# An adaLN transformer layer with circular-convolution attention and a mixture of experts: an opening and a last block in another order

## The reference, cut to what matters

```
mod = silu(c) @ wmod                     # sa, ca, ga, sb, cb, gb, each 4 x 256
ga, gb: sign kept, magnitude at least 0.25
h = layernorm(x) * (1 + ca) + sa
q, k, v = unit(h @ Wq.T + bq), unit(h @ Wk.T + bk), unit(h @ Wv.T + bv)   # unit: every Fourier coefficient divided by (its magnitude + 1e-8)
s = cumsum over tokens of fft(k) * fft(v)
x = x + ga * ifft(s * conj(fft(q)))
h = layernorm(x) * (1 + cb) + sb
gate = h @ gate_w;  top 2 of 8 experts, softmax weights
y_e = dense_2[e] @ swiglu(dense_1[e] @ h + b1[e]) + b2[e]                  # 512 hidden
x = x + gb * (weighted sum of the two y_e)
```

## Time and profile before

| | |
|---|---|
| median of 3 runs | 584.66 us (583.52 to 586.32) |
| the profiled execution: its time | 584.68 us |
| its span in the trace | 582.5 us |
| TensorE busy | 544.5 us, 93% of the span |
| VectorE busy | 473.1 us, 81% |
| ScalarE busy | 302.2 us, 52% |
| GpSimd busy | 282.8 us, 49% |

### The profile page before, as it was taken

The page is one execution under the profiler, slowest core; times in us unless marked ns, Lnnn a source line. Parts: engine busy times, 40 slices in busy tenths (PEclk is TensorE's granted clock), DMA queues, the critical chain, the costliest instruction groups (busy, mean ns, idle before and its releaser), DMA issues.

```text
span 582.5 us, 13330 instructions
## 1 busy us (share of the span) xinstructions
PE 544.5 (93%) x4008; PEld 404.8 (69%) x4009; DVE 473.1 (81%) x1062; ACT 302.2 (52%) x514; POOL 282.8 (49%) x197
## 2 busy tenths in 40 slices
PE   9999999999999985779899999999999999999992
PEld 5544555655656552537588888888888888888881
DVE  1267889999999989999688888888888888888882
ACT  4777688889797863654433333333333333333330
POOL 0004033343423342000638878877878877777634
PEclk9988999999899987858899999999999999999997
DMA  8314544644735437833677897786886686786533
GB/s 313 126 45 155 153 136 109 203 132 136 208 103 176 115 120 219 309 64 70 162 121 107 136 152 118 136 132 116 145 157 109 134 139 121 136 155 112 88 45 36
DMA packets 82109, 79.37 MB, mean 136 GB/s; under 512 B 45140, under 2 KB 71892, under 8 KB 81816
## 3 DMA queue, kind: packets, MB, share of 16 engines
q0 software_dynamic: 16912, 31.74, 31.3%
q1 hardware_dynamic: 63864, 46.28, 29.9%
q10 hardware_dynamic: 1296, 0.87, 0.5%
HBM read 44.06 MB, written 22.23 MB: 114 GB/s over the span
## 4 chain that ended last, share of the span: by engine, by line
PE 72%; DVE 13%; ACT 4%; issue 4%; DMA 4%; POOL 2%; POOLq 0%; DVEq 0%; ACTq 0%
PE ps L807 30%; PE ps L826 14%; PE ps L551 13%; PE ps L610 3%; DMA out_rows<-w_stage,region 3%; PE ps L652 2%; PE ps L564 2%; PE ps L648 2%; PE ps L474 1%; DVE region L1293 1%; POOL out_rows L1749 1%; ACT region L976 1%; PE ps L482 1%; ACT region L923 1%; DVE region L1415 1%
## 5 line engine op out<-in xcount | busy, mean ns | idle before, releaser
L807 PE MATMUL ps<-region,w_sb 128*128 128x256 f16 (+1 forms) x1920 | 194.3, 261 | 0.9 <-DMA region<-region 0.4
L807 PEld LDWEIGHTS ps<-region,w_sb 128*128 x1920 | 170.4, 98 | 20.1 <-issue 2.1
L1749 POOL DMA_INDIRECT out_rows<-w_stage,region x71 | 126.4, 1780 | 60.4 <-DMA out_rows<-w_stage,region 22.8
L1739 POOL DMA_INDIRECT region<-h_scratch,region x71 | 91.8, 1292 | 67.7 <-DVE region L1576 45.0
L1178 ACT ACTIVATE region<-region 128x1024 f16<-128x1024 f32 (+1 forms) x40 | 38.5, 961 | 130.4 <-DVE region L1630 130.4
L826 PE MATMUL ps<-region 128*128 x852 | 99.6, 273 | 1.9 <-DVE region L1636 1.7
L1622 DVE TENSOR_SCALAR region<-ps,region 128x256 f32<-128x256 f32 (+1 forms) x160 | 64.4, 448 | 43.0 <-PE ps L807 41.2
L826 PEld LDWEIGHTS ps<-region 128*128 128x128 f16 x852 | 82.6, 98 | 13.1 <-issue 3.5
L1166 ACT ACTIVATE region<-ps,region 128x256 f32<-128x256 f32 (+1 forms) x160 | 63.0, 445 | 53.0 <-PE ps L807 49.5
L551 PE MATMUL ps<-region 128*128 128x512 f32 x192 | 84.2, 595 | 3.2 <-ACT region L923 3.2
L1723 POOL TENSOR_TENSOR region<-region 128x512 f32<-128x512 f32 x30 | 37.3, 1270 | 94.9 <-DVE region L1320 94.9
(11 more groups left out here) (238 smaller groups left out, 702.3 us busy)
## 6 DMA issues: line engine op xcount, KB each, us to landing
w_stage<-in_w SPq DMA_DIRECT2D x20, 512.0 KB, 3.7
region<-in_x SPq DMA_DIRECT2D x8, 512.0 KB, 7.3
out_rows<-region SPq DMA_DIRECT2D x8, 512.0 KB, 3.0
h_scratch<-gb_bc SPq DMA_DIRECT2D x4, 1024.0 KB, 6.8
h_scratch<-region SPq DMA_DIRECT2D x8, 512.0 KB, 3.2
region<-region POOLq DMA_DIRECT2D x7, 512.0 KB, 4.5
region<-in_ramp SPq DMA_DIRECT2D x1, 2064.0 KB, 11.1
region<-in_w SPq DMA_DIRECT2D x4, 512.0 KB, 6.6
```

The source lines that it names most:

```text
L807: mm = pe.matmul(ps[:, GV + 2 * half + a, (f % 2) * MT:(f % 2) * MT + wide], w, xg_t[:, s, xa * KD + k, 0:wide], start=(n == 0), stop=(n = ...
L1739: G.indirect_dma_start(out=xg_rows[:, t % XG, u, :], out_offset=None, in_=h_scratch, in_offset=bass.IndirectOffsetOnAxis(ap=idx, axis=0)). ...
L1749: G.indirect_dma_start(out=out, out_offset=bass.IndirectOffsetOnAxis(ap=scatter_idx[:, at:at + 1], axis=0), in_=y_sb[:, t % 2, u, :], in_o ...
```

## The change

It rebuilds the opening (blocks 0 and 1) and reorders the last block.

- **Weights.** The first three chunks (EARLY = 3) are split by VectorE alone (`weight_chunk`: one scaling for the high part, one scale-and-subtract for the low). Their two ScalarE copies and six TensorE pieces go; `low_piece(0, i)` and `low_piece(1, 0)`, `(1, 1)` no longer exist. SyncE may load chunks 2 to 4 before the modulation table is written.
- **Block 0.** The magnitudes are added in three parts as the squares come (`first_magnitude`), the roots of k and v are taken between the copies (`first_root`), and VectorE adds the small constant. `modulation` runs after the `uk` product of `bind(0)` instead of before its reciprocal. ScalarE writes sb and 1 + cb already scaled by 8, which takes two VectorE instructions of `modulation` away.
- **Block 2** (the third) is normalised while block 0 is still being transformed; its transposes stand right behind `nyquist_sums(0)` on TensorE. `unbind(0)` now stands inside `bind(1)`, ahead of block 1's reciprocal; `project(1)` stands ahead of `modulation_rows` on TensorE, and `inverse(0)` behind both pieces that are left.
- **Last block.** TensorE adds x with two 512-column matmuls ahead of the wait for `unbind`; the high and low parts go to a buffer of their own (`last_parts`), so `last_split` waits for no store and no transposes; `last_residual(0)` comes before `split_rows(6)`, and `low_piece(8, 3)` and the splits of chunks 18 and 19 come later; VectorE does `last_moments(0)` before `low_rows(6)` and `top2(5)` after `last_low`. The masks of `picks` are set by GpSimd (`masks`), and the softmax weights are computed among the index steps.

The diff, cut to its core:

```diff
-            items += [("ny", 0, 0), ("lo", 0, 0)]
+            items.append(("ny", 0, 0))
+            continue
         elif t == 0:
-            items += [("pre", 0, 0), ("ny", 1, 0), ("row", 0, 0), *(("lo", 1, i) for i in range(4))]
+            items += [("ny", 1, 0), ("pre", 0, 0), ("lo", 1, 2), ("row", 0, 0), ("lo", 1, 3)]
...
-            for n in range(2):
+            for n in range(5):
                 load_weights(sp, n)
-            sp.wait_ge(mod_ready, 6)
+            sp.wait_ge(mod_ready, 4)
+            sp.wait_ge(mod_scaled, 2)
             sp.dma_start(mod_tab, mod_rows.bitcast(I32)).then_inc(mod_out, 16)
             sp.wait_ge(mod_out, 16)
             sp.dma_start(mod_bc.bitcast(I32), mod_tab[:, 0:3, :].partition_broadcast(P)).then_inc(mod_in, 16)
             sp.dma_start(gb_bc[:].bitcast(I32), mod_tab[0:2, 3, :].partition_broadcast(P)).then_inc(gb_in, 16)
-            for n in range(2, 6):
-                load_weights(sp, n)
+            load_weights(sp, 5)
...
+                if t == LAST:
+                    for h in range(2):
+                        pe.matmul(ps[:, OUT + h, :], ident_sb[:],
+                                  x_sb[:, t % XS, 2 * h:2 * h + 2, :].rearrange("p j d -> p (j d)"),
+                                  start=True, stop=False)
                 for j in range(TPB):
                     cols = ps[:, OUT + j // 2, (j % 2) * D:(j % 2 + 1) * D]
-                    if t == LAST:
-                        pe.matmul(cols, ident_sb[:], x_sb[:, t % XS, j, :], start=True, stop=False)
...
                     nyquist_cols(0)
+                    project(1)
                     modulation_rows()
-                    project(1)
-                    low_piece(0, 0)
+                    continue
                 elif t == 0:
                     transform(1)
+                    nyquist_cols(1)
                     nyquist_sums(0)
-                    nyquist_cols(1)
+                    project(2)
+                    low_piece(1, 2)
                     nyquist_row(0)
-                    low_piece(1, 0)
-                    low_piece(1, 1)
+                    low_piece(1, 3)
                     inverse(0)
-                    low_piece(1, 2)
-                    low_piece(1, 3)
                     continue
                 elif t + 1 < NBLK:
-                    project(t + 1)
+                    if t >= 2:
+                        project(t + 1)
...
-                low_piece(t + 1, 3)
+                if t < LAST:
+                    low_piece(t + 1, 3)
...
+            def modulation_rows(half):
+                act.wait_ge(mod_mm, half + 1)
+                act.wait_ge(unit_set, 2)
+                plain, scaled = ((0, 1), (3, 2))[half]
+                rows = ps[0:BATCH, OUT + half, :].rearrange("b (m d) -> b m d", m=2)
+                nc.scalar.activation(mod_rows[:, plain, :], rows[:, plain - 2 * half, :], ACT.Copy).then_inc(mod_copied, 1)
+                nc.scalar.activation(mod_rows[:, scaled, :], rows[:, scaled - 2 * half, :], ACT.Identity, scale=SX,
+                                     bias=scale_shift[0:BATCH, half:half + 1]).then_inc(mod_scaled, 1)
...
-                    if c == 2 and t == 1:
-                        split_weights(2)
                     act.wait_ge(z_ready, 6 * t + 2 * c + 2)
                     nc.scalar.activation(sq[:, c], z[:, t % 2, c, :, 0:BLK], ACT.Square).then_inc(sq_ready, 1)
+                    if t == 0 and c >= 1:
+                        first_root(c - 1)
+                    if t == 1 and c == 0:
+                        split_weights(EARLY)
                     if c == 0 and t >= 3:
                         residual(t - 2)
-                if t == 1:
-                    split_weights(3)
...
+            def first_root(c):
+
+                act.wait_ge(mag_part, c + 1)
+                nc.scalar.activation(mag[:, 0, c, 0:BLK], mag[:, 0, c, 0:BLK], ACT.Sqrt).then_inc(root_part, 1)
+
+            def first_roots():
+
+                act.wait_ge(ny_out, 1)
+                nc.scalar.activation(mag[:, 0, :, BLK:NB], mag[:, 0, :, BLK:NB], ACT.Sqrt).then_inc(root_part, 1)
+                act.wait_ge(mag_ready, 1)
+                nc.scalar.activation(mag[:, 0, QRY, 0:BLK], mag[:, 0, QRY, 0:BLK], ACT.Sqrt).then_inc(root_ready, 1)
...
-                act.wait_ge(h2_out, 16 * LAST)
-                act.wait_ge(tp2_done, KD * LAST)
-                nc.scalar.activation(h2_parts[:, 2 * h:2 * h + 2, HI, :], x2[:, 2 * h:2 * h + 2, :],
+                nc.scalar.activation(last_parts[:, 2 * h:2 * h + 2, HI, :], x2[:, 2 * h:2 * h + 2, :],
...
-                    split_weights(0)
-                    roots(0)
-                    split_weights(1)
-                    modulation_rows()
+                    first_roots()
                     spectra(1)
-                    low_piece(0, 0)
+                    modulation_rows(0)
+                    normal_rows(2)
+                    modulation_rows(1)
+                    continue
                 if t == 0:
-                    project(2)
-                    normal_rows(2)
-                    low_piece(1, 0)
-                    low_piece(1, 1)
+                    roots(1)
+                    low_piece(1, 2)
                     nyquist_row(0)
-                    roots(1)
+                    spectra(2)
+                    low_piece(1, 3)
+                    split_weights(4)
                     residual(0)
-                    low_piece(1, 2)
-                    low_piece(1, 3)
-                    spectra(2)
-                    split_weights(4)
                     split_weights(5)
                     continue
                 if t >= 2:
                     gate_rows(t - 2)
                 if t >= 1 and t + 2 < NBLK:
                     project(t + 2)
+                if t == LAST:
+                    low_piece(t + 1, 1)
+                    gate(t - 2)
+                    std2(t - 1)
+                    low_piece(t + 1, 2)
+                    nyquist_row(t)
+                    last_residual(0)
+                    split_rows(t - 1)
+                    last_residual(1)
+                    last_std(0)
+                    low_piece(t + 1, 3)
+                    split_weights(2 * t + 4)
+                    last_std(1)
...
+            def weight_chunk(n):
+
+                dve.wait_ge(w_in[stage_of(n)], 16 * arrivals(n))
+                hi, lo = parts_of(n)
+                V.tensor_scalar(hi, staged(n), SW, None, ALU.mult).then_inc(chunk_hi, 1)
+                dve.wait_ge(chunk_hi, n + 1)
+                V.scalar_tensor_tensor(out=lo, in0=staged(n), scalar=SW, in1=hi, op0=ALU.mult,
+                                       op1=ALU.subtract).then_inc(w_lo[n % 2], 2)
+
+            def first_magnitude(c):
+
+                dve.wait_ge(sq_ready, c + 1)
+                V.tensor_tensor(mag[:, 0, c, 0:BLK], sq[:, c, RE, :], sq[:, c, IM, :],
+                                ALU.add).then_inc(mag_part if c < QRY else mag_ready, 1)
...
+                if t == 0:
+                    dve.wait_ge(root_part, 3)
+                    V.tensor_scalar(mag[:, s, VAL, :], mag[:, s, VAL, :], EPS_UNIT, None, ALU.add).then_inc(eps_ready, 1)
                 dve.wait_ge(eps_ready, t + 1)
                 V.scalar_tensor_tensor(out=den, in0=mag[:, s, KEY, :], scalar=EPS_UNIT, in1=mag[:, s, VAL, :],
                                        op0=ALU.add, op1=ALU.mult).then_inc(den_ready, 1)
                 if t == 0:
-                    modulation()
+                    dve.wait_ge(root_ready, 1)
                 dve.wait_ge(den_ready, t + 1)
                 V.scalar_tensor_tensor(out=rec, in0=mag[:, s, QRY, :], scalar=EPS_UNIT, in1=den,
                                        op0=ALU.add, op1=ALU.mult).then_inc(all_ready, 1)
+                if t == 1:
+                    unbind(0)
                 dve.wait_ge(all_ready, t + 1)
                 V.reciprocal(rec, rec).then_inc(rec_ready, 1)
                 dve.wait_ge(rec_ready, t + 1)
                                 ALU.mult).then_inc(uq_ready, 1)
                 V.tensor_tensor(uk, z[:, s, KEY], mag[:, s, KEY, :].unsqueeze(1).to_broadcast([P, 2, NB]),
                                 ALU.mult).then_inc(uk_ready, 1)
+                if t == 0:
+                    modulation()
...
-            for t in range(-1, NBLK):
-                if 0 <= t < NBLK:
-                    bind(t)
-                if t >= 1:
-                    residual(t - 1)
-                if t >= 0 and t + 2 < NBLK:
+            ln1_rows(1)
+            ln1_moments(2)
+            for c in range(3):
+                weight_chunk(c)
+                if c == 0:
+                    ln1_rows(2)
+                first_magnitude(c)
+            bind(0)
+            magnitudes(1, slice(KEY, QRY))
+            magnitudes(1, slice(QRY, QRY + 1))
+            nyquist_apply(0)
+            for t in range(1, NBLK):
+                bind(t)
```

(40 more changed lines are left out.)

111 lines of the change are left out of this document (60 added, 51 removed).

## The result

The changed kernel takes 580.74 us (median of 11 runs, 580.04 to 584.07) against 586.32 us (11 runs, 583.52 to 590.1): a ratio of 0.9915, 95% interval 0.9894 to 0.9937. It is faster, by 0.85% where 1.5% was forecast, and the time lies just above the range of 573.0 to 580.5. The profiled execution took 580.04 us, with a span of 578.2 against 582.5. The kernel before is also slower in these 11 runs than in the 3 that the forecast started from (584.66).

A forecast was written before the change was run, and what follows sets the result against it. TensorE and VectorE were taken as both full in steady blocks, leaving gains in the opening and the last block's VectorE chain. 584.68 - 7.0 (opening) - 1.6 (last block) = 576.1 us, range 573.0 to 580.5.

The forecast's parts named there:

- Transform of block 1: TensorE's opening: without four low pieces, 4.3 us, transform(1) starts at 36.3 instead of 40.62 and ends at 46.8.
- VectorE in the opening: Blocks 0 and 1: three chunks take 5.4 us, block 0's reciprocal starts at 33.0 instead of 39.35, sums end at 47.3.
- The way to `inverse(0)`: Opening, from block 1's squares on: magnitudes end 49.6, `unbind(0)` runs 53.4 to 55.6, transform(2) starts 59.5, 7.0 us earlier.
- half clock or the port: Rival: where TensorE is on the path, half clock, port delay or chunk 5 costs time, giving 578 to 579.6; chance 0.13.
- The Trainium skill's rule: Opening: the last magnitudes could wait out one 1.24 us GpSimd instruction, starting transform(2) 0.8 us later than the sum.
- Waits of the new order: Opening: the modulation table delays nothing, with `gate_basis(0)` at 54.0 and wanted by `inverse(0)` at 54.5, slack 0.5 us.
- chunk 5: Weight load issued at 59 us: a landing of up to 5.5 us costs nothing, one of 10.1 costs 4.5.
- third of the forecast's own signs of being wrong: Steady blocks: the forecast is wrong if the lead of 7 us shrinks from block to block.
- the first two: Opening signs of error: VectorE waits on weight DMA between 22 and 30 us, or `inverse(0)` waits for GpSimd.
- Last block: VectorE's closing chain shortens by 1.6 us, bounds -0.4 and 2.3; `last_low` comes another 1.3 us earlier.
- From there on nothing changes: Behind the last block: the rest of the kernel neither gains nor loses time.
- The range: Whole kernel: 573.0 to 580.5 us, taking in the forecast and two rivals, 0.88 less its edges.

The follow-up runs named there:

- late transform: The changed kernel with 19 idle matmuls ahead of transform(1), as long as the low pieces the change removed there; 582.34 us, ratio 0.9908 to the kernel before.
- opening alone: The changed kernel with the last block's part taken back, the opening kept; 582.43 us, ratio 0.9919 to the kernel before.
- split product: The changed kernel with VectorE doing two of the four products of block 0 that GpSimd did; first time 577.77 us, ratio 0.9854 to the kernel before.
- split product with the fill at the gather: The split product plus 12 idle matmuls behind the gather's issue, none ahead of inverse(0); 577.76 us, ratio 0.9860 to the kernel before.
- both fills: The changed kernel with idle matmuls both ahead of inverse(0) and behind the gather's issue; 579.41 us, ratio 0.9880 to the kernel before.
- fill at the inverse: The changed kernel with 18 idle matmuls in TensorE's gap ahead of inverse(0); 580.43 us, ratio 0.9895 to the kernel before.
- repeat of the split product: The split product run again unaltered, in a later group; 580.49 us, ratio 0.9903 to the kernel before.

## Why the prediction was wrong

The direction was right, and so was VectorE's part of the opening. The steps that failed are three terms of the sum: den(1) and its successor were taken from a stretch without GpSimd beside them (1.3 us), the inverse was taken at full clock behind a gap (1.67 us), and the entry of the expert loop was put at nothing (1.7 us).

- **Transform of block 1**, forecast 36.3: it came at 34.22. The 4.3 us of the pieces are there; the rest is luck of the two traces: the modulation rows ran at full clock (3.60 us; 5.29 before), and transform(0) began 0.4 earlier. In four of the eleven traces with the changed opening those rows took 4.4 to 5.0 us, and transform(1) began at 35.9 to 36.6. The early start was worth little, as the late transform showed: the magnitudes of block 1 then waited for VectorE's own running sums, done at 46.5, and not for the squares.
- **VectorE in the opening.** Chunk 2 was done at 28.7 (forecast 29.0), the reciprocal at 32.3 (33.0), the sums at 46.5 (47.3), the magnitudes of block 1 at 49.3 (49.6). All held, though the terms given for the reciprocal (0.7, 0.7 and one product of 0.69 behind 29.89) add to 32.0 and not 33.0, and the 1.22 us of the earlier trace rows was no form slowed by GpSimd: the chunks took 1.22 us with GpSimd idle. VectorE's reciprocal of block 1 is 8.15 us earlier, 8.6 in the forecast.
- **The way to `inverse(0)`.** Here are the first two failed terms. From the magnitudes' end to `unbind(0)` the sum took 3.8 us from a stretch without GpSimd beside it, although in the same sum GpSimd's product ran until 52.3, beside most of it; it was 5.1 (49.3 to 54.43), because den(1) and its successor took 1.1 and 0.3 us more. `unbind(0)` itself was 0.5 us shorter than the 2.2 forecast and ended at 56.15 instead of 55.6. Then the 3.1 us of the inverse were 4.77 at the half clock. 0.55 + 1.67 = 2.2 of the 2.3 us missing at transform(2). The forecast placed TensorE's waiting "twice, 2 to 3 us in all" ahead of the inverse; it was one of 4.53. The rival "half clock or the port" had the right mechanism, with 578 to 579.6 us and 0.13; it deserved to be the forecast, since the forecast's own gap was one of its conditions. Its range was still too low, because it too had no half clock at the expert loop.
- **The Trainium skill's rule** weighed there ("SBUF — State Buffer", section "SBUF: two separate sides"), that a VectorE instruction with two SBUF inputs can be held by GpSimd for a whole instruction, agrees in direction with this trace: den(1) was 1.12 us over its 0.69, and one GpSimd product takes 6.24 / 4 = 1.56. The forecast had priced it, at 0.8 us, for the last magnitudes alone. Those were in time (49.3); the delay fell on the two products behind them, 1.3 us.
- **Waits of the new order.** The modulation table's write was issued at 41.80 (forecast 42.2), its broadcast at 43.54, and `gate_basis(0)` was done at 55.0, 0.6 us ahead of the inverse. No wait on it, nor on chunk 5.
- **The lead between blocks.** It shrank by 0.57 us from transform(2) to transform(7), by a lapse of the clock to 0.93 in one steady block. A shrinking lead was the third of the forecast's own signs of being wrong; the first two did not show. The forecast took the earlier trace rows's clock of 1.00 for all of them, while the kernel before also had one block at 0.93 (140.14 to 166.24, 26.10 us).
- **Last block**, forecast 1.6: 1.57 at the gather's issue. `last_low` is 1.5 us earlier beyond the lead, forecast 1.3. The third failed term is the sentence "From there on nothing changes": behind the gap ahead of the gathered tile, 2.42 us where it was 1.95, chunk 23's low parts ran at half clock and gave 1.7 us back. In effect this part was worth next to nothing in the traces: 0.3 us gained without the new opening, 0.35 lost with it.
- **The range.** Its lower end of 573.0 follows from no bound that is given: the best case of the last block, 2.3 us, reaches 575.4.

The sum by its own steps is then 7.0 - 2.3 - 0.6 = 4.1 in the blocks, + 1.6 - 1.7 + 0.3 (a gather that landed sooner) = 4.3, the difference of the spans.

What stays open is why the clock falls in steady blocks in which TensorE is busy, in some executions and not in others, and whether a half clock removed in one place comes back in another. The traces lean that way. From transform(2) to transform(7) it took 125.4 us in three of the four traces with the half clock at `inverse(0)` (126.9 in the opening alone), and 126.2 to 126.9 in six of the seven in which that inverse ran at full clock or nearly (124.8 in the first trace of the split product). That would be 1 of the 1.7 us given back. With one trace of each execution it is not shown that one lapse causes the other.

**The best version** was the split product with the fill at the gather, 577.76 us and 0.9860 [0.9823, 0.9897], against 0.9915 [0.9894, 0.9937] for the change in its own 11 runs: some 3 us, with intervals that just overlap. The split product alone had 577.77 and 580.49, the latter in the same group as the best version, and those intervals overlap too. The best of many is also in part the luckiest, so the fill's own share is not shown by the medians.

## What to carry to other kernels

When an order frees an engine, write down the length of every gap that it leaves on TensorE, and price the work right behind each gap at half clock as well as at full: here 1.7 us at each of two places, at the second all that the edit there had brought. Take the duration of an operation from a stretch in which the same neighbours run, since den(1) was 0.69 us alone and 1.81 beside GpSimd. A gap can be closed by moving needed work into it, which cost nothing here; idle matmuls help where they end before the gap does, and get in the way where the gap has become shorter. An earlier start is worth what reaches the next step: 4.15 us at transform(1) were worth some 0.8 at transform(2).

## What was not expected of the hardware

- The granted clock fell to 0.81 to 0.84 over 70 to 80 us while TensorE was busy in all of it (both fills). Four of the eleven kernels above have this longer step from transform(2) to (3), by 1.5 to 1.7 us.
- A gap did not decide by itself. Gaps of 4.5 us were followed by half clock in all three traces that had one, and so was the one of 3.08 us. After 2.74 us the split product's row work ran at full clock in one trace (0.60 us) and its next pair at half clock in another (1.92 us for the pair otherwise of 1.02). At the expert loop gaps of 1.49 and 1.95 us cost nothing, while those of 1.92 (fill at the inverse) and 1.93 (the repeat of the split product) cost 1.3 us in the low parts and 0.4 in the matmuls behind them.
- Two products of 512 columns on VectorE beside GpSimd's work took 1.40 us each (0.69 alone), while GpSimd's own, beside VectorE's, took 1.89 us each, against 1.24 in the kernel before: both engines lose.
